# An interaction network whose products are formed with field pairs on partitions instead of samples, so that no product tile is transposed

## The chip, the cores and the metric

The kernel runs on one core of a Trainium2 chip. The metric is device time in microseconds (us), the median of several runs. The engines are named as in the profile: PE is TensorE (matmul), PEld its weight loads, DVE is VectorE, ACT is ScalarE, POOL is GpSimd, SP is SyncE, which here only issues DMAs. All data is float32. A product of two float32 matrices is made from float32r matmuls: each operand is split into a high part (rounded to float32r) and a low part (the rest).

## The reference

1024 samples, 39 fields each. `inputs` is [1024, 39, 16]: an embedding row looked up in a table, times the field's value. With h = `inputs` at first, three layers are computed, each for every embedding column d (16 of them):

```
x = einsum('bhd,bmd->bhmd', h, inputs).reshape(B, -1, 16)   # all pairs (h, m)
x = relu(einsum('bcd,oc->bod', x, W_i) + b_i)               # 200 outputs
h, direct = x[:, :100], x[:, 100:]                          # last layer: direct = x
```

The first layer has 39*39 pairs (the kernel uses their symmetry: 780), the second and third 100*39 = 3900 each. The `direct` parts are summed over d and dotted with `fc_W`. Beside it a dense network 624 -> 400 -> 400 with relu runs on the flat inputs, is dotted with the rest of `fc_W`, and a bias per looked-up row is added. The output is one score per sample.

## The kernel before

The samples are cut into 8 tiles of 128, and each tile into its 16 columns d: 128 chunks. A chunk's layer is a matmul with the products as the stationary operand, [pairs on partitions, 128 samples], and the weights as the moving one; it needs 7 tiles of 128 pairs in layer 0 and 31 tiles in each of layers 1 and 2.

POOL forms the products with the samples on partitions (`product0`, `product`), so they have the wrong orientation for the matmul. Layer 0 products are transposed on PE (`turn_group`); those of layers 1 and 2 on DVE, in blocks of 32 x 32 (`turn_group` of the DVE program, L719). For that h and the inputs are held "quartered": 32 samples on each quarter of the partitions, which ACT prepares with 16 small copies per layer (`quarter`, L598).

A transposed group (4 tiles, 128x512) lies in PSUM. ACT copies it to `xhi` (`high`, L582), DVE subtracts to get `xlo` (`low`, L725), and PE does two matmuls per tile (`multiply_group`): L524, xhi against [high | low] weights, 400 columns, and L525, xlo against the high weights, 200 columns. One group each of layers 1 and 2 is left "whole": 4 tiles by plain float32 matmuls (L516). `low_copy`, `add` and `dot` clear an accumulator and feed the next layer.

Every engine runs one hand-written order. In step i they do layer 0 of chunk i+1, layer 1 of chunk i and layer 2 of chunk i-1 (`step_groups`), with rings of 4 buffers. POOL also gathers the next sample tile's 39 embedding rows, 2 or 3 indirect DMAs at the head of each step (`gathers`, L364), and scales them once a tile. After the last chunk comes the dense network.

Of the kernel before, what the change touches and what calls it, by code (L numbers as in the profile page):

```python
# [55 lines left out]
SPLIT_GROUPS = [GROUPS[0], GROUPS[1] - 1, GROUPS[2] - 1]  # L77
STEP = sum(SPLIT_GROUPS)
LAST = CHUNKS - 1
DENSE_STEP = GROUPS[FIRST] + GROUPS[SECOND]  # L80
CIN_GROUPS = STEP * CHUNKS
assert STEP % RING == 0 and DENSE_STEP % RING == 0


def first_group(i):

    return 2 * SPLIT_GROUPS[0] + SPLIT_GROUPS[1] + STEP * (i - 1)


def dense_group(i):  # L90

    return CIN_GROUPS + GROUPS[FIRST] + DENSE_STEP * (i - 1)


SLOT = first_group(1) % RING
DENSE_SLOT = dense_group(1) % RING


def groups_of(job, c):
    return [(job, c, q) for q in range(GROUPS[job])]  # L100


def whole(job, q):

    return job in (1, 2) and q == WHOLE[job]


def splits_in(groups):
    return sum(1 for job, c, q in groups if not whole(job, q))
# [7 lines left out]
L0_DONE = 4  # L117
L1_DONE = 9


def dense_groups(i):
    return groups_of(FIRST, i) + groups_of(SECOND, i - 1)


def group_tiles(job, q):

    return range(SIZE[job] * q, min(SIZE[job] * (q + 1), len(ROWS[job])))


def group_parts(job, q):  # L130

    parts = []
    for t in group_tiles(job, q):
        at = (t % SIZE[job]) * P
        if parts and parts[-1][0] == ROWS[job][t]:
            parts[-1] = (parts[-1][0], slice(parts[-1][1].start, at + P))
        else:
            parts.append((ROWS[job][t], slice(at, at + P)))
    return parts


def weights_at(layer, t):

    before = sum(KT[n] - (GROUP if WHOLE[n] is not None else 0) for n in range(layer))
    skipped = WHOLE[layer] is not None and t >= GROUP * (WHOLE[layer] + 1)
    return (before + t - (GROUP if skipped else 0)) * 2 * OUTS


def start_groups():
    return groups_of(0, 0) + groups_of(0, 1) + groups_of(1, 0)  # L150


def is_first(c):
    return isinstance(c, int) and c == 0


def tail_groups():

    return groups_of(1, LAST) + groups_of(2, LAST - 1) + groups_of(2, LAST) + groups_of(FIRST, 0) + dense_groups(1)


def rec_kernel(nc, x_store, vals, ids, table, w0_ab, w0_ba, w1, w2, d0, d0_b, d1, d1_b, fc_w, fc_b, out):
    with ExitStack() as ctx:
# [6 lines left out]

        W = sb("W", [P, weights_at(2, KT[2])], F32R)
        w_whole = sb("w_whole", [P, 2, GROUP, OUTS], F32)
        x_whole = sb("x_whole", [P, 2, GROUP * P], F32)
        prods = sb("prods", [P, KT_ALL * P], F32)
        xhi = sb("xhi", [P, RING, GROUP * P], F32R)
        xlo = sb("xlo", [P, RING, GROUP * P], F32R)
# [79 lines left out]
        s_out = sem("output_stored")  # L256

        block = ctx.enter_context(nc.Block())

        per = STAGE // OUTS
# [649 lines left out]
```

## Time and profile before

| | |
|---|---|
| median of 3 runs | 3019.55 us (3016.03 to 3020.39) |
| the profiled execution: time, span | 3024.12 us, 3022.3 us |
| granted PE clock, mean | 0.996 |
| PE / PEld busy | 95% / 92% |
| DVE / ACT / POOL busy | 90% / 72% / 80% |
| data moved by DMA | 29.42 MB, mean 10 GB/s |

An engine's share is the time in which it ran an instruction. The span is from the first to the last instruction; the profiled execution's time is 1.8 us longer. Matmuls overlap each other, so what a matmul costs is read from the distance between two starts and not from its duration; on DVE and ACT too the next instruction starts up to 0.1 us before the last one's end.

### The profile page before, as it was taken

To read this page: it belongs to the slowest core of one execution; us is meant where nothing else is said; L and a number is where in the kernel's file an instruction comes from. 1 tells how busy PE (TensorE), PEld (TensorE's weight loads), DVE (VectorE), ACT (ScalarE), POOL (GpSimd) and SP (SyncE) were. 2 spreads that over 40 slices of the span, in tenths; PEclk is the share of its full clock that TensorE was granted. 3 is DMA by queue.
4 is the path that set the end of the run, shared out by engine and by line. 5 is a ranking of instruction groups with operands and counts; after the bars stand their busy time and mean duration, and the time that the engine had idled before them with its cause. 6 is when DMAs were issued, how large, how long until landed. Compare 5 with 4: busy or idle time off the path is not lost.

```text
span 3022.3 us, 69958 instructions
## 1 busy us (share of the span) xinstructions
PE 2883.5 (95%) x18848; PEld 2783.5 (92%) x18848; DVE 2731.5 (90%) x5355; ACT 2163.4 (72%) x6593; POOL 2417.9 (80%) x1513
## 2 busy tenths in 40 slices
PE   0799999999999999999999999999999999999998
PEld 0799999999999999999999999999999999999997
DVE  2699999999999999999999999999999999999995
ACT  2677777777777777777777777777777777777772
POOL 7788888888888888888888888888888888767660
PEclk9899999999999999999999999999999999999999
DMA  6100010000000010000100001000100001000001
GB/s 122 19 1 1 1 22 1 1 1 7 16 1 1 1 22 1 1 1 1 22 1 1 1 1 22 1 1 1 21 2 1 1 1 22 1 0 0 0 35 30
DMA packets 36455, 29.42 MB, mean 10 GB/s; under 512 B 22960, under 2 KB 28976, under 8 KB 36400
## 3 DMA queue, kind: packets, MB, share of 16 engines
q1 hardware_dynamic: 26160, 26.11, 3.8%
q0 software_dynamic: 10240, 2.81, 3.2%
q14 instruction: 48, 0.39, 0.0%
q8 instruction: 7, 0.11, 0.0%
HBM read 26.33 MB, written 2.56 MB: 10 GB/s over the span
## 4 chain that ended last, share of the span: by engine, by line
ACT 30%; issue 29%; DVE 29%; PE 6%; DVEq 2%; ACTq 2%; POOL 2%; DMA 1%; SPq 0%; POOLq 0%
DVE xlo L725 15%; ACT h2q L598 10%; ACT h1q L598 10%; ACT xhi L582 10%; DVE turn L719 7%; DVE acc_sum L735 4%; PE acc L524 2%; DVE x_whole L719 2%; POOL raw L364 1%; DVEq L723 1%; ACTq L580 1%; PE acc L525 1%; DVE spent L742 1%; PE turn L496 1%; PE acc L516 1%
## 5 line engine op out<-in xcount | busy, mean ns | idle before, releaser
L524 PE MATMUL acc<-W,xhi 128*128 128x400 f32 x7808 | 2437.0, 374 | 61.3 <-DVE xlo L725 36.0
L525 PE MATMUL acc<-W,xlo 128*128 128x200 f32 x7808 | 1990.3, 255 | 0.0
L524 PEld LDWEIGHTS acc<-W,xhi 128*128 128x128 f32 x7808 | 1467.5, 188 | 154.5 <-DVE xlo L725 153.5
L725 DVE TENSOR_TENSOR xlo<-turn,xhi 128x512 fp32r<-128x512 f32 (+1 forms) x2088 | 1341.7, 648 | 223.7 <-ACT xhi L582 194.6
L525 PEld LDWEIGHTS acc<-W,xlo 128*128 128x128 f32 x7808 | 1492.1, 191 | 0.0
L582 ACT ACTIVATE xhi<-turn 128x512 fp32r<-128x512 f32 (+1 forms) x2088 | 1165.4, 571 | 397.9 <-PE acc L525 216.2
L414 POOL TENSOR_TENSOR prods<-h1q,xq 128x1092 f32<-128x1092 f32 (+2 forms) x512 | 933.1, 1854 | 413.7 <-ACT h1q L598 407.2
L719 DVE STREAM_TRANSPOSE turn<-prods 128x512 f32<-128x512 f32 (+1 forms) x1792 | 1244.9, 695 | 18.3 <-POOL prods L414 13.3
L414 POOL TENSOR_TENSOR prods<-h2q,xq 128x1092 f32<-128x1092 f32 (+2 forms) x512 | 934.1, 1854 | 12.6 <-ACT h2q L598 12.6
L598 ACT ACTIVATE h1q<-acc_sum 32x25 f32<-32x25 f32 x2048 | 456.2, 223 | 242.5 <-DVE acc_sum L735 215.1
L598 ACT ACTIVATE h2q<-acc_sum 32x25 f32<-32x25 f32 x2048 | 456.9, 223 | 76.9 <-DVE acc_sum L735 49.6
L516 PE MATMUL acc<-w_whole,x_whole 128*128 128x200 f32 x2048 | 393.0, 335 | 0.0
L364 POOL DMA_INDIRECT raw<-table,idx x320 | 313.4, 979 | 89.4 <-issue 82.3
L516 PEld LDWEIGHTS acc<-w_whole,x_whole 128*128 128x128 f32 x2048 | 336.4, 190 | 0.0
L397 POOL TENSOR_TENSOR prods<-xin 128x780 f32 (+1 forms) x128 | 215.5, 1684 | 5.2 <-POOL idx L359 3.1
L496 PE MATMUL turn<-ident,prods 128*128 128x128 f32 (+1 forms) x928 | 146.0, 275 | 69.1 <-POOL prods L397 67.8
L589 ACT ACTIVATE acc_lo<-acc 128x200 f32<-128x200 f32 x384 | 129.2, 337 | 96.7 <-PE acc L525 96.7
L719 DVE STREAM_TRANSPOSE x_whole<-prods 128x512 f32<-128x512 f32 x256 | 177.3, 693 | 0.0
L496 PEld LDWEIGHTS turn<-ident,prods 128*128 128x128 f32 (+1 forms) x928 | 105.6, 141 | 71.7 <-issue 68.3
L735 DVE TENSOR_TENSOR acc_sum<-acc,acc_lo 128x200 f32<-128x200 f32 x384 | 135.2, 352 | 10.4 <-ACT acc_lo L589 10.4
L742 DVE SCALAR_TENSOR_TENSOR spent<-acc_sum,fcp 128x100 f32<-128x100 f32 (+1 forms) x384 | 105.5, 275 | 0.1
L742 DVE DVE_READ_ACCUMULATOR spent<-acc_sum,fcp (+1 forms) x384 | 32.6, 85 | 0.0
(44 smaller groups left out, 227.5 us busy)
## 6 DMA issues: line engine op xcount, KB each, us to landing
xq<-x_store SPq DMA_DIRECT2D x32, 312.0 KB
raw<-table,idx POOLq DMA_INDIRECT x320
prods<-w SPq DMA_DIRECT2D x9, 500.0 KB, 7.8
x_store<-xin SPq DMA_DIRECT2D x8, 312.0 KB
raw<-x_store SPq DMA_DIRECT2D x8, 312.0 KB, 2.9
prods<-d SPq DMA_DIRECT2D x1, 1000.0 KB, 4.8
w_whole<-w SPq DMA_DIRECT2D x2, 400.0 KB, 12.8
prods<-d SPq DMA_DIRECT2D x1, 800.0 KB, 6.5
```

Source lines behind the costliest of these rows:

```text
L364: nc.gpsimd.indirect_dma_start(out=raw[:, m * EMB_COLS:(m + 1) * EMB_COLS], out_offset=None, in_=table, in_offset=bass.IndirectOffsetOnAxi ...
L397: nc.gpsimd.tensor_tensor(prods[:, 0:PAIRS].rearrange("p (s a) -> p s a", a=FIELDS), x[:, 0:FIELDS].unsqueeze(1).broadcast_to([P, SHIFTS, ...
L414: nc.gpsimd.tensor_tensor(out[:, :, a * FIELDS:b * FIELDS].rearrange("p q (h m) -> p q h m", m=FIELDS), hq[layer - 1][:, :, a:b].unsqueeze ...
L496: mm = pe.transpose(turn[slot][0:rows, at:at + P], src[:, t * P:t * P + rows], ident[:])
L516: mm = pe.matmul(bank[:, 0:OUTS], x_whole[:, job - 1, at:at + P], w_whole[:, job - 1, t % GROUP, :], start=False, stop=False, skip_group_c ...
L524: pe.matmul(bank[:, 0:2 * OUTS], hi, w, start=start, stop=end, skip_group_check=True)
L525: mm = pe.matmul(bank[:, 0:OUTS], lo, w[:, 0:OUTS], start=False, stop=end, skip_group_check=True)
L582: op = nc.scalar.activation(xhi[0:rows, slot, cols], turn[slot][0:rows, cols], ACT.Copy)
L598: op = nc.scalar.activation(hq[layer][QUARTER * i:QUARTER * (i + 1), q, :], acc_sum[QUARTER * q:QUARTER * (q + 1), layer, H_QUARTER * i:H_ ...
L719: nc.vector.transpose(place.rearrange("p (t q s) -> p t q s", q=4, s=QUARTER), src.rearrange("p q (t k) -> p t q k", k=QUARTER)).then_inc( ...
L725: op = nc.vector.tensor_tensor(xlo[0:rows, slot, cols], turn[slot][0:rows, cols], xhi[0:rows, slot, cols].bitcast(F32), ALU.subtract)
L735: nc.vector.tensor_tensor(acc_sum[:, layer, :], acc[layer][:, 0:OUTS], acc_lo[:, layer, :], ALU.add).then_inc(s_acc[layer], 1)
```

## The change

The products are now formed with the pairs on partitions: partition p holds h number p, and the free dimension runs over fields m and samples. Both factors have to be spread for it.

The inputs go through memory. DVE turns a scaled tile (`turn_inputs`), SP stores it by field (`store_inputs`, to `xs`), and from there reads it back for each chunk so that every partition gets the same rows: 96 partitions read the same 4 KB, 32 others a second piece (`load_block`, four blocks per chunk into `xrep`, double-buffered), and `load_layer0`. That is 31 x 128 samples x 4 bytes on each of 128 partitions for a chunk, 2.03 MB, and 0.48 MB more for layer 0. The dense network reads its inputs by field, too. The weights are rearranged to the new order of rows through memory at the start.

h needs one transpose on PE per layer and chunk (`turn`), between two copies on ACT: `take` before it and `spread` (six activations) behind it.

The groups are shared out. Two of 4 tiles per layer ("P", 3 tiles in the second one of layer 0) are multiplied and made low by POOL, six more per layer ("D") by DVE, with the product in PSUM; ACT makes every high part. All tiles are split now and the whole groups are gone; a tile that holds the left-over rows has its low part on its own spare partitions and needs one matmul of 400 columns. Rings: 3 buffers for P, 4 for D, 3 PSUM banks.

```
-def step_groups(i):
-    l0, l1 = groups_of(0, i + 1), groups_of(1, i)
-    return l0[:1] + l1[:3] + l0[1:] + l1[3:] + groups_of(2, i - 1)
+ORDER = [("P", 0), ("D", 0), ("D", 1), ("P", 1), ("D", 2), ("D", 3), ("P", 2), ("D", 4), ("D", 5), ("P", 3),
+         ("D", 6), ("D", 7), ("P", 4), ("D", 8), ("D", 9), ("P", 5), ("D", 10), ("D", 11)]
...
+            def load_block(c, buf, e):      # SP
+                sp.dma_start(xrep[0:H_MAIN, buf, t0:t0 + n, :].rearrange("p t n -> p (t n)"),
+                             field_rows(c, t0, n).partition_broadcast(H_MAIN)).then_inc(s_xblk[e], 16)
...
+            def low(i, k):                  # POOL; product(i, par, k) writes prod_p
+                n, slot, cols = p_num(i, k), p_slot(i, k), len(tiles_of("P", k)) * P
+                pool.wait_ge(s_hi_p, n + 1)
+                nc.gpsimd.tensor_tensor(xlo_p[:, slot, 0:cols], prod_p[:, slot, 0:cols],
+                                        xhi_p[:, slot, 0:cols].bitcast(F32), ALU.subtract).then_inc(s_lo_p, 1)
...
+                for at, k in enumerate(mine):            # POOL, one step
+                    if at + 1 < len(mine):
+                        product(i, par, mine[at + 1])
+                    elif ahead is not None:
+                        product(i + 1, 1 - par, ahead)
+                    low(i, k)
...
+            with pool.Fori(0, TILES - 1) as k:
+                for j in range(DIM):
+                    gathers(j)
+                    if j == FREE_AT:
+                        scale(k + 1, True)
+                        copy_idx((k + 2) % TILES, k + 3)
+                    step(k * DIM + (j + 2), j % 2, 0)
...
+                for kind, g in step_order(i):            # PE, one step
+                    multiply(i, kind, g)
+                    if (kind, g) == ("D", 1) and not (isinstance(i, int) and i < 1):
+                        turn(1, i - 1, i - 1)
+                    if (kind, g) == ("D", 7) and 0 in layers:
+                        turn(0, i + 1, i)
...
+            def spread(l, c, i):            # ACT
+                act.wait_ge(s_turn[l], c + 1)
+                h = hrep[l][:, 0, :]
+                nc.scalar.activation(hrep[l][0:H_MAIN, 2:4, :],
+                                     h[0:H_MAIN, :].unsqueeze(1).broadcast_to([H_MAIN, 2, P]), ACT.Copy)
+                nc.scalar.activation(hrep[l][H_MAIN:P, 3, :], h[QUARTER:2 * QUARTER, :], ACT.Copy)
+                nc.scalar.activation(hrep_s[l][0:H_MAIN, :], h[0:H_MAIN, :], ACT.Copy)
+                nc.scalar.activation(hrep_s[l][H_MAIN:P, :], h[0:QUARTER, :], ACT.Copy)
+                nc.scalar.activation(hrep[l][H_MAIN:P, 2, :], h[2 * QUARTER:3 * QUARTER, :], ACT.Copy)
+                nc.scalar.activation(hrep[l][0:P - 4, 1, :], h[0:P - 4, :], ACT.Copy).then_inc(s_hrep[l], 1)
...
+                    if (kind, g) == ("D", 3) and 1 in layers and inner:    # ACT, behind high(i, kind, g)
+                        spread(1, i - 1, i - 1)
+                    if (kind, g) == ("D", 9) and 0 in layers:
+                        spread(0, i + 1, i)
```

Two places of the order matter for what follows. On POOL, before, the boundary of two steps (h1q and h2q are h of layers 1 and 2, quartered; the DMAs are the gathers):

```order
L414 TENSOR_TENSOR prods<-h2q,xq 128x4x234 [waits turned2]
L414 TENSOR_TENSOR prods<-h2q,xq 128x4x195 [waits turned2]
L364 DMA raw<-table,idx 128x17 x2
L393 ISA
L397 ISA [waits turned0]
L397 TENSOR_TENSOR prods<-xin 128x780
L403 ISA
L412 ISA [waits h1_quartered]
L414 ISA [waits turned1]
L414 TENSOR_TENSOR prods<-h1q,xq 128x4x273
L412 REGISTER_ALU
```

And now, at the same boundary (prod_p<-l0x 128x512 is group P0 of the next step, 128x384 is P1; xlo_p is the low part, first of P4, then of P5, and last of P0):

```order
L529 REGISTER_ALU
L530 TENSOR_TENSOR xlo_p<-prod_p,xhi_p 128x512 [waits p_high]
L510 ISA
L517 ISA [waits layer0_inputs_loaded]
L524 TENSOR_TENSOR prod_p<-l0x 128x512 [waits p_low]
L529 REGISTER_ALU
L530 TENSOR_TENSOR xlo_p<-prod_p,xhi_p 128x512 [waits p_high]
L484 DMA raw<-table,idx 128x17 x2
L517 REGISTER_ALU
L524 TENSOR_TENSOR prod_p<-l0x 128x384 [waits p_low]
L529 REGISTER_ALU
L530 TENSOR_TENSOR xlo_p<-prod_p,xhi_p 128x512 [waits p_high]
```

The gathers still stand at the boundary, but the low parts of P5 and P0 now stand around them, and each waits for ACT's high part.

On ACT, before, behind the low copy of layer 0, where h goes to layer 1:

```order
L586 REGISTER_ALU
L589 ACTIVATE acc_lo<-acc 128x200 [waits acc_summed0,split_group_multiplied]
L594 REGISTER_ALU
L596 REGISTER_ALU [waits acc_summed0]
L598 ACTIVATE h1q<-acc_sum 32x25 [waits products1]
L598 ACTIVATE h1q<-acc_sum 32x25 x3
L578 REGISTER_ALU
L582 ACTIVATE xhi<-turn 128x384 [waits split_group_multiplied,turned1]
L598 ACTIVATE h1q<-acc_sum 32x25 [waits products1,acc_summed0]
```

And now, from the high part of D9 on (hrep and hrep_s are h as spread, waiting for PE's transpose; then the high parts of P5 and D10, and `take` of layer 1):

```order
L738 ACTIVATE xhi_d<-prod_d 128x512 [waits d_multiplied,d_products]
L768 ACTIVATE hrep<-hrep 96x256 [waits p_products,h1_turned]
L770 ACTIVATE hrep<-hrep 32x128
L771 ACTIVATE hrep_s<-hrep 96x128
L772 ACTIVATE hrep_s<-hrep 32x128
L773 ACTIVATE hrep<-hrep 32x128
L774 ACTIVATE hrep<-hrep 124x128
L729 REGISTER_ALU
L732 ACTIVATE xhi_p<-prod_p 128x512 [waits p_multiplied,p_products]
L735 REGISTER_ALU
L738 ACTIVATE xhi_d<-prod_d 128x512 [waits d_multiplied,d_products]
L757 ACTIVATE hbuf<-acc 128x96 [waits h2_turned,fc_dotted1]
```

The high part of P5 now stands behind six copies that wait for a transpose on PE; before, the copies of h waited for DVE's sum only and stood between groups.

## Rows read from the trace of the kernel before

**Rows 1.** Stretch, us; busy of PE, PEld, DVE, ACT, POOL; clock; DMA share; GB/s.

```profile
10.00:20.00 10.00, 0.00 (x0) 0.00 (x0) 8.50 (x9) 6.21 (x8) 8.12 (x7) 1.00 0.98 262
40.00:60.00 20.00, 0.00 (x0) 0.00 (x0) 0.00 (x0) 0.00 (x0) 15.12 (x17) 1.00 0.20 7
107.00:2944.00 2837.00, 2796.02 (x18375) 2704.19 (x18373) 2654.51 (x5198) 2110.95 (x6472) 2340.78 (x1441) 1.00 0.05 6
2944.00:3022.30 78.30, 65.58 (x366) 58.47 (x364) 42.70 (x101) 23.37 (x58) 3.66 (x3) 0.94 0.10 29
```

**Rows 2.** Waits of the steady part, 107 to 2944 us: total, times, longest.

```profile
POOL prods L414 <- ACT h1q L598: 403.0, 123, 7.4
...
PEld acc L524 <- DVE xlo L725: 131.9, 380, 2.5
```

**Rows 3.** Timeline of PE in the steady part: start us, us, then what ran.

```profile
1504.52 1.53 PE L516 MATMUL acc<-w_whole,x_whole 128*128 128x200 f32 x8
1505.75 0.48 PE L524 MATMUL acc<-W,xhi 128*128 128x400 f32 x1
...
1518.64 0.49 PE L496 MATMUL turn<-ident,prods 128*128 128x128 f32 x3
1518.88 0.43 PE L524 MATMUL acc<-W,xhi 128*128 128x400 f32 x1
...
1522.17 0.36 PE L524 MATMUL acc<-W,xhi 128*128 128x400 f32 x1
1522.37 0.26 PE L525 MATMUL acc<-W,xlo 128*128 128x200 f32 x1
...
1525.10 0.36 PE L524 MATMUL acc<-W,xhi 128*128 128x400 f32 x1
...
1526.86 1.54 PE L516 MATMUL acc<-w_whole,x_whole 128*128 128x200 f32 x8
```

**Rows 4.** Timeline of DVE, same stretch.

```profile
1499.92 0.67 DVE L725 TENSOR_TENSOR xlo<-turn,xhi 128x512 fp32r<-128x512 f32 x1
1500.52 0.68 DVE L719 STREAM_TRANSPOSE x_whole<-prods 128x512 f32<-128x512 f32 x1
...
1518.84 0.35 DVE L735 TENSOR_TENSOR acc_sum<-acc,acc_lo 128x200 f32<-128x200 f32 x1
```

**Rows 5.** Timeline of ACT, same stretch.

```profile
1503.23 0.93 ACT L598 ACTIVATE h1q<-acc_sum 32x25 f32<-32x25 f32 x4 [1.70 <-DVE acc_sum L735]
...
1509.14 0.33 ACT L589 ACTIVATE acc_lo<-acc 128x200 f32<-128x200 f32 x1
1509.36 0.61 ACT L582 ACTIVATE xhi<-turn 128x512 fp32r<-128x512 f32 x1
...
1519.24 0.50 ACT L582 ACTIVATE xhi<-turn 128x384 fp32r<-128x384 f32 x1 [0.67 <-PE turn L496]
```

**Rows 6.** Groups of POOL instructions by shape: busy us, mean ns of one.

```profile
L414 POOL TENSOR_TENSOR prods<-h1q,xq 128x1092 f32<-128x1092 f32 x256 | 520.0, 2053 | 413.7 <-ACT h1q L598 407.2 <-DMA xq<-x_store 6.5
...
L397 POOL TENSOR_TENSOR prods<-xin 128x780 f32 x125 | 210.5, 1684 | 4.8 <-POOL idx L359 3.1
L414 POOL TENSOR_TENSOR prods<-h1q,xq 128x780 f32<-128x780 f32 x128 | 194.7, 1521 | 0.0
...
L374 POOL TENSOR_TENSOR xin<-raw,val 128x624 f32 x7 | 13.1, 1873 | 0.0
```

**Rows 7.** Timeline of POOL, same stretch as ACT.

```profile
1499.73 1.53 POOL L414 TENSOR_TENSOR prods<-h2q,xq 128x780 f32<-128x780 f32 x1
...
1504.93 1.69 POOL L397 TENSOR_TENSOR prods<-xin 128x780 f32 x1
...
1516.28 7.23 POOL L414 TENSOR_TENSOR prods<-h2q,xq 128x1092 f32<-128x1092 f32 x4
...
1525.92 1.68 POOL L397 TENSOR_TENSOR prods<-xin 128x780 f32 x1
```

**Rows 8.** Chain of waits in the start-up: start us, us, what.

```profile
67.64 8.38 DMA x_store<-xin
```

More of the change, by code:

```diff
@@ L130, in group_parts @@
[L130 to L146, printed above, removed]
@@ L344, in _ @@
+            sp.wait_ge(s_prod_p, p_num(CHUNKS, 5) + 1)
+            sp.wait_ge(s_prod_d, d_num(CHUNKS, 11) + 1)
+            for tile in range(2, TILES):
                 load_dense(tile)
@@ L533, in multiply_group @@
-                mm.then_inc(s_mmw[job] if whole(job, q) else s_mm, 1)
-            def run(n0, slot0, groups, ahead, fresh=False, distance=2):
-                following = groups + ahead
-                def turn_ahead(g):
-                    if g < len(following) and following[g][0] not in (1, 2):
-                        before = splits_in(following[:g])
-                        turn_group(n0 + before, (slot0 + before) % RING, *following[g])
-                if fresh:
-                    for g in range(2):
-                        turn_ahead(g)
-                for g in range(len(groups)):
-                    turn_ahead(g + distance)
-                    before = splits_in(groups[:g])
-                    multiply_group(n0 + before, (slot0 + before) % RING, *groups[g])
+                        mm = split_tile(acc[layer], hi, lo, w, start, end)
@@ L588, in low_copy @@
+            def low_copy(layer, c, i):
+                if layer == 2:
+                    act.wait_ge(s_mm_d, d_num(i, 11) + 1)
+                else:
+                    act.wait_ge(s_mm_p, p_num(i, 1 + 2 * layer) + 1)
+                if some(c):
                     act.wait_ge(s_acc[layer], c)
@@ new lines, in step @@
+            def step(i, par, ahead):
+                layers, mine = present(i), d_groups(i)
+                for at, d in enumerate(mine):
+                    if at + 2 < len(mine):
+                        product(i, par, mine[at + 2])
+                    elif at + 2 - len(mine) < len(ahead):
+                        product(i + 1, 1 - par, ahead[at + 2 - len(mine)])
+                    low(i, d)
+                    if d == 3 and 1 in layers and not (isinstance(i, int) and i < 2):
+                        evacuate(2, i - 2)
+                    if d == 5 and 0 in layers:
+                        evacuate(0, i + 1)
+                    if d == 9 and 1 in layers:
+                        evacuate(1, i)
+                if layers == (0, 1):
+                    evacuate(1, i)
@@ new lines, in _ @@
+            with dve.Fori(0, TILES - 1) as k:
+                for j in range(DIM):
+                    if j == 8:
+                        turn_inputs(k + 1, True)
+                    step(k * DIM + (j + 2), j % 2, [0, 1])
+            for i in range(2 + DIM * (TILES - 1), CHUNKS):
+                step(i, i % 2, d_groups(i + 1)[0:2] if i < LAST else [])
+            evacuate(2, LAST - 1)
+            product(CHUNKS, 0, d_groups(CHUNKS)[0])
+            product(CHUNKS, 0, d_groups(CHUNKS)[1])
```

1132 lines of the change are left out of this document (654 added, 478 removed).

## The prediction

> **What bounds the kernel now.** I read the busy time by stretch first, then the waits of the steady part, then the timelines of one step. In the steady part, 107 to 2944 us, PE is busy 2796 of 2837 us, DVE 2655, POOL 2341, ACT 2111 [rows 1]; the largest wait is POOL's for h1q, 403 us, and PE's weight loads wait 132 us for DVE's low parts [rows 2]. So PE is nearly full, and DVE is close behind it. One step is the distance between the two whole groups of layer 1, 1504.52 and 1526.86: 22.34 us [rows 3]. What PE needs for it comes from distances of starts: ten pairs (L524, L525) take 1525.10 - 1522.17 = 2.93 us, 0.293 a pair; a whole group takes 1505.75 - 1504.52 = 1.23; three transposes 0.24 [rows 3]. 61 pairs, two whole groups and seven transposes make 17.9 + 2.5 + 0.6 = 20.9 us, and 1.4 us a step are gaps.
>
> **What PE does after the change.** 67 pairs (7 + 30 + 30), two matmuls of 400 columns without a partner at 0.20 each (1522.37 - 1522.17), and two transposes at 0.08: 19.6 + 0.4 + 0.2 = 20.2 us [rows 3]. The work removed (two whole groups and five transposes, 2.5 + 0.4) is nearly paid back by six more pairs and the two lone matmuls (1.8 + 0.4). If nothing else counted, a step would lose 2.1 us.
>
> **What the other engines do.** DVE: 24 instructions of 512 elements or fewer, 0.60 us apart at most (1499.92 to 1500.52), and three evacuations of an add, 0.35, and a dot of the like [rows 4]: 14.4 + 2.1 = 16.5 us. That a product reads and writes PSUM is shown by no row; the nearest are the subtraction and the transpose of the same size at 0.67 and 0.68, and DVE has 4 us to spare, so I cost it at nothing. ACT: 18 high parts at 0.6 or less, three low copies at 0.33, four copies in `take` and twelve in `spread`. Four copies of 25 elements took 0.93 and a copy of 200 let the next start after 0.22 [rows 5], so 0.23 each: 10.8 + 1.0 + 3.7 = 15.5 us. POOL: twelve instructions of 512 or 384 elements. No row has that size. Rows 6 give 2053 ns for 1092 and 1521 for 780 elements, 1.7 ns an element and 0.19 us fixed, so 1.06 us; the product of layer 0, both inputs streaming, 1684 for 780, gives 1.17; the strided scaling, 1873 for 624, gives 3.0 ns an element and 1.54. The new operands are contiguous; I take 1.1 and keep 1.0 and 1.54 as ends. With 2.44 gathers at 1.25 a step that is 13.2 + 3.0, about 16.5 with the scaling. Each engine has less to do than PE's 20.2. What decides is then the order.
>
> The GPSIMD Engine Reference of the Trainium skill (3.1, Elementwise — side-by-side cycle accounting) says that a two-input `tensor_tensor` on this engine costs about 2.6 cycles an element at 1.2 GHz. The rows give 1.7 to 1.9 ns where the rule gives 2.2. By the rule one instruction would be 1.27 us, an estimate from that page, and the sum 3270 us.
>
> **The wait that the change adds.** Count from the moment when PE has issued D7 and turns h1 (t = 0). ACT's `spread` waits for that transpose, the high part of P5 is queued behind it on ACT, and POOL's low part of P5 behind that. Transpose 0.4 (three took 0.49 [rows 3]), six copies 6 * 0.23 + 0.1 = 1.5, high part 0.6 [rows 5], low part 1.1, and three hand-overs at 0.1 (transposes end at 1519.13, ACT starts at 1519.24 [rows 3, 5]): P5 is ready at 3.9. Meanwhile PE has P4, D8 and D9, 12 pairs, 3.5 us. Gap 0.4.
>
> Behind the low part of P5 POOL has the gathers of the next step, the product of P1, and only then the low part of P0, with which PE begins the next step. Three gathers take from 1501.26 (1499.73 + 1.53) to 1504.93, 3.67 us, two from 1523.51 to 1525.92, 2.41 [rows 7]. So P0 is ready at 3.9 + 3.67 + 2 * 1.1 + 0.1 = 9.9, or 8.6 with two gathers, or 6.2 with none. PE wants it after P5, D10 and D11, ten pairs and a lone matmul: 3.9 + 2.9 + 0.2 = 7.0. Gap 2.9, 1.6 or none. Nothing catches it up: the next turn again waits for PE's own D7, so a gap of one step is not made good in the next.
>
> The turn of h2 has the same chain to P2: ready at 3.9, while PE has only P1, D2 and D3, 11 pairs, 3.2. Gap 0.7. For the other groups I walked the same orders and found the low parts about 1 us or more ahead of PE (P3 is the closest).
>
> Steps: 20.2 + 0.4 + 0.7 = 21.3 without gathers, 22.9 with two, 24.2 with three. Of 16 steps of a sample tile nine have three and six have two (39 gathers over 15 steps); the last has the scaling, one of 1.87 [rows 6], one of about half that, and small ones, 3.9 in all, so 24.4. Mean (9 * 24.2 + 6 * 22.9 + 24.4) / 16 = 23.7, against 22.34 now.
>
> **The DMAs.** SP issues 14 a step. They bring 2.03 + 0.48 = 2.5 MB; at the 262 GB/s of the start-up, where the queues are 98% full [rows 1], that is 9.6 us of 23.7. Each block is asked for some five D groups, about 8 us, before its first product, and a block of 0.52 MB takes 2 us to move, so I cost them at nothing. Their limit: below 2.5 MB / 23.7 us = 106 GB/s they become the bound. They also share the engines with the gathers. With the queues 98% full 7 gathers were issued in 10 us, 1.43 each, against 17 in 20 us in the quiet stretch, about 1.2 [rows 1]. At half load that is at most 0.1 per gather; I leave it in the range.
>
> **Start and end.** Full steps are 126 before and after. The rest is now 3022.3 - 126 * 22.34 = 207 us. The end keeps its work (the last groups, the dense layers; 78.3 us from 2944 [rows 1]). The start gets longer. All 7.7 MB of weights go to memory in the new order and come back: 15.4 MB at 262 GB/s are 59 us, beside the first gathers, which end at about 60 anyhow. Then the inputs are stored in 3840 pieces of 128 bytes, where 2048 pieces of 156 took 8.4 us [rows 8], so 7 us more; 22 instead of 4 DMAs spread them and the layer-0 and block loads follow, 9 more; and the halves of layers 1 and 2 (6200 columns each, at DVE's 0.60 / 512 some 7 us) are now made between the first steps, 14 us. I take 30, with 0 and 60 as ends.
>
> **Sum.** 112 steps of the loop with gathers, 14 without (the first one and the last sample tile's): 112 * 23.7 + 14 * 21.3 + 207 + 30 = 2654 + 298 + 237 = 3189 us of span. The profiled execution was 1.8 us over its span and 4.6 over the median, so 3186; I say 3185. Ends: POOL's 1.0 instead of 1.1 shortens a step by 0.4 us and the start by up to 30, giving 3110; gathers at 1.35 and the longer start give 3250. With the hand-overs 0.1 either way the likeliest case has 3080 to 3290.
>
> **Rivals.**
> - *The gathers stay hidden* (faster). POOL runs ahead far enough that its 3 to 4 us at the step boundary don't reach PE: 126 * 21.3 + 237 = 2921 us, or 2820 if the turns cost nothing either. For it: every engine's load is under 17 of 20.2 us, and the gathers before were harmless beside a POOL that waited 403 us [rows 2]. Against it: the low part of P5 cannot be made before `spread`, by the rows of the order. The break-even step is (3022 - 237) / 126 = 22.1 us, a mean gap of 1.9 where I count 3.5; half of my error would do. Chance 0.30, a third of it between 2921 and 3013.
> - *POOL is dearer than thought* (slower still). At 1.54 us per instruction three of them stand on the way to P0, two of them new behind the gathers, and one on the way to P2: 25.5 us with gathers, 22.3 without, 112 * 25.5 + 14 * 22.3 + 237 = 3405. For it: the scaling's row; against: its inputs are strided. Chance 0.11.
> - *The broadcast reads are slow* (slower). 16 queues read the same 4 KB; no row of before shows that in a steady stream. At 90 GB/s a step would last 28 us and the kernel 126 * 28 + 237 = 3765. Chance 0.04.
> - *No change within what can be told* (0.2%, 6 us): 0.03, where gains and gaps happen to cancel.
>
> **How the numbers follow.** My forecast has 0.52. Slower by over 0.2%: 0.52 + 0.11 + 0.04 = 0.67; faster 0.30; the same 0.03. Below 2920 lie about 0.1 and above 3380 about 0.1, so the range is 2920 to 3380.
>
> **What the profile after would show.** Right: PE waits for POOL's xlo_p, some 300 us in all; the step is 24 us with three gathers and near 21.3 in the last sample tile, which has none, and this difference is the clearest sign. POOL is idle before the low part of P5 and busy behind it. ACT's first hrep copy waits for PE's transpose twice a step. POOL's 512-element instructions take 1.0 to 1.2 us; DMA is near half busy. Wrong: steps with and without gathers equally long; PE waiting for DVE's xlo_d, which would mean that the product in PSUM is slow; DVE or POOL waiting for xrep; a first full step later than 180 us. If the steps with gathers are under 22 us, the forecast fails, most likely at the walk from the turn to P0.

## The result, and the profile after

The changed kernel takes 3377.57 us (median of 4 runs, 3369.05 to 3378.28); the kernel before, on the same chip, 3019.97 (3016.03 to 3020.49). The ratio is 1.118, 95% interval 1.116 to 1.120. The forecast was 3185 us, with a range of 2920 to 3380: the sign was right, the time lies at the upper end of the range, and the kernel lost 358 us where 165 were forecast. The profiled execution has a span of 3375.5 us.

First the busy time by stretch, with the columns of [rows 1]. The first line is the steady part (from the first full step to the last), the others look into one step.

```profile
169.00:3307.00 3138.00, 2743.98 (x17504) 2649.58 (x17503) 2195.05 (x4442) 1738.54 (x4684) 2122.18 (x1817) 0.97 0.41 107
...
1515.00:1520.00 5.00, 3.38 (x21) 3.12 (x21) 4.55 (x8) 1.53 (x4) 4.25 (x5) 1.00 0.16 6
1520.00:1522.00 2.00, 1.02 (x3) 1.03 (x4) 1.18 (x3) 1.46 (x4) 2.00 (x2) 0.63 0.30 89
1522.00:1524.00 2.00, 2.00 (x9) 1.99 (x9) 1.32 (x5) 0.00 (x0) 2.00 (x3) 0.50 0.51 150
1524.00:1526.00 2.00, 2.00 (x9) 1.99 (x8) 0.00 (x0) 0.00 (x0) 0.29 (x1) 0.50 0.00 2
1526.00:1528.00 2.00, 2.00 (x12) 2.00 (x11) 0.00 (x0) 0.08 (x1) 0.00 (x0) 0.66 0.00 0
1528.00:1530.00 2.00, 2.00 (x16) 2.00 (x16) 0.34 (x1) 1.92 (x7) 0.00 (x0) 1.00 0.00 0
```

PE was busy 2796 of 2837 us before and is busy 2744 of 3138 now. No engine is full, so the order decides. What PE has to do is what the forecast said (e2 below has steps of 20.18 us); the gaps are larger. The last column but two has something new: behind the gap at 1518 to 1521 us the granted clock is 0.50, that is 1.2 GHz, for 6.8 us.

The waits of the whole execution (total, times, longest), which answer to [rows 2]:

```profile
POOL xlo_p L530 <- ACT xhi_p L732: 911.7, 252, 12.5
ACT hrep L768 <- PE hrep L639: 726.4, 255, 6.5
DVE prod_d L915 <- ACT hrep L774: 625.9, 247, 6.2
PE acc L606 <- POOL xlo_p L530: 528.6, 369, 110.0
...
DVE prod_d L915 <- DMA xrep<-xs: 32.4, 7, 5.1
```

Read from the bottom: DVE hardly waits for the broadcast loads. PE waits for POOL's low parts, POOL for ACT's high parts, ACT for the turn on PE, twice a step. This is the ring of the forecast.

POOL in one step with three gathers (start us, us, what; what ended the idle time), to be held against [rows 7]:

```profile
1509.16 1.29 POOL L524 TENSOR_TENSOR prod_p<-l0x 128x512 f32<-128x512 f32 x1
1513.70 1.29 POOL L530 TENSOR_TENSOR xlo_p<-prod_p,xhi_p 128x512 fp32r<-128x512 f32 x1 [3.25 <-ACT xhi_p L732]
1515.13 0.98 POOL L484 DMA_INDIRECT raw<-table,idx  x1
...
1518.62 1.01 POOL L524 TENSOR_TENSOR prod_p<-l0x 128x384 f32<-128x384 f32 x1
1519.57 1.27 POOL L530 TENSOR_TENSOR xlo_p<-prod_p,xhi_p 128x512 fp32r<-128x512 f32 x1
```

ACT in the same step: six copies of the spread, and only then the high part of P5.

```profile
1511.25 0.36 ACT L768 ACTIVATE hrep<-hrep 96x256 f32<-96x256 f32 x1 [1.63 <-PE hrep L639]
...
1512.70 0.26 ACT L774 ACTIVATE hrep<-hrep 124x128 f32<-124x128 f32 x1
1512.99 0.63 ACT L732 ACTIVATE xhi_p<-prod_p 128x512 fp32r<-128x512 f32 x1
```

And PE, from the turn to the first group of the next step:

```profile
1510.95 0.27 PE L639 MATMUL hrep<-ident,hbuf 128*128 128x128 f32 x1
...
1518.06 0.36 PE L628 MATMUL acc<-W,xhi_d 128*128 128x400 f32 x1
1520.98 0.70 PE L606 MATMUL acc<-W,xhi_p 128*128 128x400 f32 x1 [2.56 <-POOL xlo_p L530]
...
1521.64 0.59 PE L606 MATMUL acc<-W,xhi_p 128*128 128x400 f32 x1
...
1522.19 0.58 PE L606 MATMUL acc<-W,xhi_p 128*128 128x400 f32 x1
```

The reader sees the forecast's walk: P5 ready 1514.99 - 1510.95 = 4.0 us after the turn (forecast 3.9), P0 started after 10.0 (9.9), the gap 2.56 (2.9). What the forecast did not have is the distance of the pairs behind the gap: 0.55 us instead of 0.29.

The length of a step is the distance between the starts of ACT's copy L768 for h1. Two steps:

```profile
1412.44 0.36 ACT L768 ACTIVATE hrep<-hrep 96x256 f32<-96x256 f32 x1 [1.63 <-PE hrep L639]
...
1435.73 0.36 ACT L768 ACTIVATE hrep<-hrep 96x256 f32<-96x256 f32 x1 [1.63 <-PE hrep L639]
...
3165.86 0.36 ACT L768 ACTIVATE hrep<-hrep 96x256 f32<-96x256 f32 x1 [1.63 <-PE hrep L639]
...
3187.56 0.36 ACT L768 ACTIVATE hrep<-hrep 96x256 f32<-96x256 f32 x1 [1.63 <-PE hrep L639]
```

23.3 us with two gathers, 21.7 without any (in the last sample tile). I measured all steps in this way. All 42 with two gathers take 23.3 (forecast 22.9). The 63 with three take 24.5 at least (24.2), but 36 of them 26.0 to 31.0. The seven with the scaling take 26.2 to 26.4 (24.4), the last 13 21.7 (21.3). The loop's 112 steps take 2808.5 us, mean 25.08, where the forecast had 23.7.

### The profile page after: what moved, and what is told of

It reads as the page before. It is cut to its first block, busy times and chain, and to the rows that moved or that the text cites. A ratio compares the mean times of both kernels' runs of the same rounds, so it can differ in the third digit from the quotient of the medians.

```text
span 3375.5 us, 66460 instructions
## 1 busy us (share of the span) xinstructions
PE 2824.3 (84%) x17912; PEld 2723.2 (81%) x17912; DVE 2265.5 (67%) x4563; ACT 1790.0 (53%) x4774; POOL 2231.5 (66%) x1921
## 4 chain that ended last, share of the span: by engine, by line
issue 44%; POOL 39%; PE 7%; SPq 6%; DVE 2%; ACT 1%; DMA 1%; POOLq 1%; ACTq 0%; DVEq 0%
POOL xlo_p L530 17%; POOL prod_p L524 16%; POOL raw L484 5%; PE acc L606 4%; SPq L351 3%; PE acc L607 2%; DMA l0x<-xs 1%; SPq L291 1%; DVE xlo_d L923 1%; DVE prod_d L915 0%; SPq L314 0%; POOL xin L497 0%; POOLq L517 0%; SPq L301 0%; SPq L367 0%
## 5 line engine op out<-in xcount | busy, mean ns | idle before, releaser
L606 PE MATMUL acc<-W,xhi_d 128*128 128x400 f32 x5632 | 1770.5, 373 | 13.8 <-DVE xlo_d L923 11.6
L530 POOL TENSOR_TENSOR xlo_p<-prod_p,xhi_p 128x512 fp32r<-128x512 f32 (+1 forms) x768 | 953.7, 1242 | 911.7 <-ACT xhi_p L732 911.7
L915 DVE TENSOR_TENSOR prod_d<-hrep,xrep 128x512 f32<-128x512 f32 (+1 forms) x1536 | 1039.0, 677 | 719.2 <-ACT hrep L774 625.9
L607 PE MATMUL acc<-W,xlo_d 128*128 128x200 f32 x5632 | 1462.2, 260 | 0.0
L606 PE MATMUL acc<-W,xhi_p 128*128 128x400 f32 x2944 | 993.5, 388 | 528.6 <-POOL xlo_p L530 528.6
L607 PEld LDWEIGHTS acc<-W,xlo_d 128*128 128x128 f32 x5632 | 1113.6, 198 | 0.0
L606 PEld LDWEIGHTS acc<-W,xhi_d 128*128 128x128 f32 x5632 | 1095.6, 195 | 18.2 <-DVE xlo_d L923 13.3
L923 DVE TENSOR_TENSOR xlo_d<-prod_d,xhi_d 128x512 fp32r<-128x512 f32 (+1 forms) x1536 | 982.0, 639 | 170.2 <-ACT xhi_d L738 166.0
L738 ACT ACTIVATE xhi_d<-prod_d 128x512 fp32r<-128x512 f32 (+1 forms) x1536 | 886.7, 581 | 54.7 <-DVE prod_d L915 25.6
L607 PE MATMUL acc<-W,xlo_p 128*128 128x200 f32 x2944 | 764.6, 260 | 0.0
L524 POOL TENSOR_TENSOR prod_p<-hrep_s,xrep 128x512 f32<-128x512 f32 x512 | 664.8, 1298 | 15.5 <-ACT hrep L774 8.3
L768 ACT ACTIVATE hrep<-hrep 96x256 f32<-96x256 f32 x256 | 92.4, 361 | 726.4 <-PE hrep L639 726.4
L628 PE MATMUL acc<-W,xhi_d 128*128 128x400 f32 x256 | 92.6, 362 | 0.0
```

The lines of the kernel that those rows point to most:

```text
L524: nc.gpsimd.tensor_tensor(to, one.unsqueeze(1).broadcast_to([P, count, P]), many, ALU.mult).then_inc(s_prod_p, 1)
L530: nc.gpsimd.tensor_tensor(xlo_p[:, slot, 0:cols], prod_p[:, slot, 0:cols], xhi_p[:, slot, 0:cols].bitcast(F32), ALU.subtract).then_inc(s_l ...
L606: pe.matmul(bank[:, 0:2 * OUTS], hi, w, start=first, stop=last, skip_group_check=True)
L607: return pe.matmul(bank[:, 0:OUTS], lo, w[:, 0:OUTS], start=False, stop=last, skip_group_check=True)
L738: nc.scalar.activation(xhi_d[:, slot, 0:cols], prod_d[d_bank(i, g)][:, 0:cols], ACT.Copy).then_inc(s_hi_d, 1)
L915: nc.vector.tensor_tensor(to, h, xrep[:, (par + layer - 1) % 2, a:a + count, :], ALU.mult).then_inc(s_prod_d, 1)
```

## Experiments

All are changes of the changed kernel, if nothing else is said: e6 is one of the kernel before, e8 stands on e2, e9 on e8, and e10 and e12 on e9. "Steps" are measured as above, and long ones at single places of the loop are told in the text.

| run | median us | ratio to before (95%) | steps: two / three gathers / none, us | 112 loop steps, us |
|---|---|---|---|---|
| changed kernel | 3377.57 | 1.116 to 1.120 | 23.3 / 24.5+ / 21.7 | 2808.5 |
| e11 no second rewrite | 3372.05 | 1.110 to 1.118 | 23.3 / 24.5+ / 21.7 | 2826.9 |
| e4 clock kept | 3341.73 | 1.104 to 1.108 | 23.3 / 24.5 / 23.3 | 2758.9 |
| e13 short product | 3289.92 | 1.087 to 1.091 | 22.8 / 24.0+ / 21.7 | 2719.8 |
| e1 gathers moved | 3165.21 | 1.046 to 1.050 | 21.7 / 22.1 / 21.7 | 2590.6 |
| e5 no gathers | 3076.37 | 1.017 to 1.020 | - / - / 21.7 | 2502.7 |
| e7 h1's high part first | 3043.54 | 1.006 to 1.009 | 21.1 / 21.3 / 21.1 | 2476.0 |
| e3 both edits | 3024.27 | 1.001 to 1.002 | 20.2 / 21.2 / 20.2 | 2474.1 |
| e2 both high parts first | 2935.27 | 0.970 to 0.973 | 20.2 / 20.4 / 20.2 | 2384.6 |
| e8 stores split | 2878.72 | 0.952 to 0.955 | 20.2 / 20.4 / 20.2 | 2326.2 |
| e10 gathers late | 2877.38 | 0.952 to 0.955 | 20.2 / 21.0 / 20.2 | 2335.1 |
| e9 start reordered | 2864.57 | 0.948 to 0.951 | 20.2 / 20.4 / 20.2 | 2323.3 |
| e12 first gathers late | 2848.31 | 0.942 to 0.944 | 20.2 / 20.4 / 20.2 | 2302.2 |

**e1: the gathers at another place of POOL's row.**

```
-    gathers(j)
     ...
-    step(k * DIM + (j + 2), j % 2, 0)
+    step(k * DIM + (j + 2), j % 2, 0, lambda: gathers(j))   # called ahead of low(i, 5)
```

> POOL issues the gathers of the loop just ahead of its low part of P5, where it stands idle for 3.25 us in the trace after, instead of just ahead of the product of P1. Theory (the gathers lie behind the spread on the way to P0, and the gap lets PE's clock fall): the low part of P0 is ready 2.4 to 3.7 us earlier in the steps with gathers, they fall from 25.1 us in the mean to 21.5 to 22.5, and granted clocks of 0.50 in the loop go; 112 * 3.1 = 350 us less, about 3030 us, with 2960 and 3130 as ends. Rival A (every gather costs by what it moves or by load on the DMA queues, wherever it stands): steps stay at 24 to 25, 3330 to 3380. Rival B (the dearer POOL instructions bind by their sum): steps about 24, over 3250.

3165 us. Steps with two gathers fell from 23.3 to 21.7, with three from 24.5 to 22.1: two gathers vanish in POOL's idle 3.25 us, three stick out of it by 0.4. The fallen clock goes from all of these; 16 stretches at 0.50 are left in the loop, instead of 43, behind its 16 long steps. Rivals A and B are out. These 16 steps of 28.6 to 30.9 us are also why the total missed the theory's 3030 (ends 2960 and 3130): seven are those of the scaling, which now waits for the rows of gathers that were issued later (14.8 us in all), seven wait for the layer-0 rows (46.0 us, see e8), and in two a gather stands 6 us (see e12).

**e2: the spread behind the high part.**

```
-    if (kind, g) == ("D", 3) and 1 in layers and inner:
+    if (kind, g) == ("P", 2) and 1 in layers and inner:
         spread(1, i - 1, i - 1)
-    if (kind, g) == ("D", 9) and 0 in layers:
+    if (kind, g) == ("P", 5) and 0 in layers:
         spread(0, i + 1, i)
```

> ACT makes the high part of P2 ahead of the spread of h2, and that of P5 ahead of the spread of h1, instead of behind them; the gathers stay where they are. Theory (the spread pins the low part of P5, and all of POOL's row behind it): POOL makes the low part of P5 some 2.3 us earlier, so the gathers and the low part of P0 come 2.3 us earlier too, and the gap at P2 goes; steps with three gathers about 22 to 22.5, with two about 21.5, no fall of the clock; about 3040 us, with 2970 and 3140 as ends. Rival (the hrep copies come so late now that the products wait for them, or POOL's sum binds): steps stay over 23.5, over 3200.

2935 us, 85 less than the kernel before, and below the theory's ends (2970 and 3140). The gathers stand where they stood, and all but 15 steps of the loop take 20.2 to 20.7 us: just what the forecast gave PE to do, 20.2. The rival, steps over 23.5, is out. POOL of this kernel, around the gathers that end at 1508.2:

```profile
1508.18 1.02 POOL L524 TENSOR_TENSOR prod_p<-l0x 128x384 f32<-128x384 f32 x1
1509.15 1.29 POOL L530 TENSOR_TENSOR xlo_p<-prod_p,xhi_p 128x512 fp32r<-128x512 f32 x1
...
1522.37 1.30 POOL L524 TENSOR_TENSOR prod_p<-l0x 128x512 f32<-128x512 f32 x1
1523.63 1.29 POOL L530 TENSOR_TENSOR xlo_p<-prod_p,xhi_p 128x512 fp32r<-128x512 f32 x1
1525.07 0.98 POOL L484 DMA_INDIRECT raw<-table,idx  x1
```

The low part of P5 follows the product without the 3.25 us of idle time, before the turn of h1 is even spread (ACT's copy L768 starts at 1524.42); the theory had it 2.3 us earlier, and it no longer waits for the turn at all. So the two pinned low parts, of P2 and P5, were the whole loss of the changed kernel against the kernel before, and more.

**e3: both edits.**

> Both edits at once: gathers ahead of the low part of P5, and the high parts of P2 and P5 ahead of the spreads. Theory: no gap at the boundary is left, the step is what PE needs plus small gaps, 20.5 to 21.3 us with and without gathers; 126 * 20.9 + 263 = 2900, with 2850 and 2970 as ends, faster than the kernel before. Rival (one edit alone already takes all that can be had): the same as the better of the two single edits. Rival (another bound stands at 22 to 23 us, by POOL's sum or DMA): over 3030.

3024 us: worse than e2 alone. None of the three cases came: neither the theory's 2900, nor the better of the two single edits, nor a step of 22 to 23 us. What I had not written is this: when the low part of P5 is no longer late, three gathers ahead of it make it late (21.2 us a step instead of 20.4), and the scaling waits as in e1 (28.0 to 29.2 us instead of 20.7, 55 of the 90 us that the loop loses against e2). A place that is free in one order isn't free in the other.

**e7: only the spread of h1 behind.**

> Only the spread of h1 goes behind the high part of P5; the spread of h2 stays ahead of the high part of P2. Theory: P0 comes in time, the gap at P2 stays; by the forecast that gap is 0.7 us, by the trace after it is a part of the 1.5 us between 21.7 and 20.2, so steps of 20.9 to 21.4 with and without gathers, no fall of the clock but at the stalls: 2935 + 126 * 0.9 = 3050 us, with 3020 and 3090 as ends. Rival (the gap at P2 is the larger one and its delay runs on into the next turn): over 3150. Rival (the gap at P2 costs nothing once P0 is in time): 2935 to 2950.

3043.5 us, as the theory had it (3050); of the 442 us of e2, 334 come from this half of the edit alone. Without gathers a step is 21.13 us. Against 20.18 in e2 and 21.69 in the changed kernel this prices the two gaps of the forecast: at P2 0.95 us (forecast 0.7), at P5 0.56 (0.4).

**e5 and e6: the loop's gathers left out, after and before.**

```
 for j in range(DIM):
-    gathers(j)
```

> The changed kernel without the gathers of its loop (those ahead of the loop stay; the inputs of most later sample tiles are then stale). Theory (in the loop the gathers stand behind the pinned low part of P5, on the way to P0, and the clock falls behind the gaps they make): all 126 full steps last 21.7 us as the last 13 do in the trace after, save the ones where SP or POOL stalls at the loop's boundary; 112 * 3.4 = 380 us less, 3000 us, with 2980 and 3050 as ends. Rival (the last steps are short because no block or store of a later tile is loaded beside them, and the gathers are innocent): steps over 23, over 3150.

> The kernel before without the gathers of its loop. Theory (there POOL had slack and nothing waited behind the gathers): no more than 30 us less than before, 2990 to 3020. Rival (the gathers cost in both kernels, the change only added a constant): 150 us or more less, under 2870.

After: 3076 us, 301 less. Before: 3019.4 against 3019.3, ratio 0.9988 to 1.0007: nothing. The waits of before without gathers say why; POOL's wait for h1q is 745 us instead of the 403 to 407 of [rows 2, 6], so all that the gathers took was idle time:

```profile
POOL prods L416 <- ACT h1q L599: 745.4, 127, 7.4
```

So the same gathers are free in one kernel and cost 300 us in the other. The forecast had 112 * 23.7 - (105 * 21.3 + 7 * 24.4) = 247 us for them. The e5 total is 76 above the 3000 I expected, and above the end of 3050, since 20 steps of its loop take 22.8 to 27.9 us: seven with the scaling, seven in which POOL waits for the layer-0 rows, and six at the head of a pass of the loop. These seven with the rows are 30 us over the usual here; in the changed kernel they are only 6 us over it, so there the gaps of the gathers covered most of that wait.

**e4: the gap filled with matmuls without effect.**

```
+    if (kind, g) == ("P", 0) and not isinstance(i, int):
+        pe.wait_ge(s_hbuf[0], i + 1)
+        for _ in range(14):
+            pe.matmul(acc[0][:, 2 * OUTS:512], ident_r[:, 0:P], ident_r[:, 0:112],
+                      start=False, stop=False, skip_group_check=True)
     multiply(i, kind, g)
```

> Everything as in the changed kernel, but in the loop PE issues 14 matmuls of 112 columns on data without effect ahead of P0, before it waits for the low part of P0 (the results of layer 0 are not the reference's, since the accumulator's unused columns are written). Theory (a part of the time is not the gap itself but PE's clock of 0.50 behind it): the granted clock stays at 1.00 in the loop, the steps of 24.9 us and more at j other than 0 fall to 24.5 or a little less, 80 to 120 us less, about 3280. Rival (the clock is no cause, the long steps come from something else, such as DMA latency of the gathers): within 20 us of 3377.

3341.7 us, 36 less, not 80 to 120. Two things are in it. In the loop the steps with three gathers that had taken 26 to 27.5 us take 24.5, save seven at 26.1: 45 us less. The seven with the scaling fall from 26.3 to 24.7: 11 us less. The others lose 2 and gain 8, so the 112 steps take 49.6 us less, and the stretches at 0.50 are 17 instead of 43. PE's own loop goes on into the last sample tile, and in 12 of its steps, which have no gathers, the 14 matmuls stand in the way and cost 1.6 us each, some 19 us. In this stretch of e4 the gap is filled and the clock stays at full speed:

```profile
1520.00:1530.00 10.00, 9.67 (x69) 9.43 (x69) 8.39 (x16) 4.72 (x12) 8.96 (x8) 1.00 0.38 88
```

So the fallen clock is a cause of its own, worth 56 us at least in these steps (the long ones at the head of a pass took 29.5 to 30.6 us here too).

**e13: one POOL instruction shorter.**

```
-    a, count = tiles[0], len(tiles)
+    a, count = tiles[0], 1 if k == 1 and not isinstance(i, int) else len(tiles)
```

> The changed kernel, but in the loop POOL forms only the first 128 of the 384 columns of the product of P1 (the others keep what stood there, so layer 0 is not the reference's). This instruction stands behind the gathers and ahead of the low part of P0, took 1.01 us and should take about 0.4. Theory (in the steps with gathers each us on that row is a us of the step, in those without it is none): steps with three gathers fall from 24.5 to 23.9, with two from 23.3 to 22.7, the last 13 stay at 21.7; 112 * 0.6 = 67 us, and with the gap at 2.0 instead of 2.6 us some of the 50 us that the fallen clock costs goes too: 3377 - 90 = 3287 us, with 3255 and 3312 as ends. Rival (POOL's instructions are not the limit there, what they wait for is): under 20 us.

3290 us; the forecast of the theory was 3287. Its instruction, before (of the changed kernel) and in e13, from the groups by shape:

```profile
L524 POOL TENSOR_TENSOR prod_p<-l0x 128x384 f32<-128x384 f32 x128 | 129.6, 1012 | 3.5 <-POOL idx L479 1.7
```

```profile
L524 POOL TENSOR_TENSOR prod_p<-l0x 128x128 f32<-128x128 f32 x112 | 52.4, 468 | 3.5 <-POOL idx L479 1.7
```

0.54 us less, and the steps with gathers lose 0.55 each, so on this row a us of POOL is a us of the step. Over the 112 steps that is 62 us of the 89 that the loop lost; the stretches at 0.50 are 31 instead of 43. What the edit says nothing of is the steps without gathers: in the last 13, which stay at 21.7, the product was not shortened (112 of 128 were). That a shorter instruction on another row would be worth nothing, no run here tests.

**e8: SP's stores in portions.** In e2 every 16th step still took 28.1 to 28.9 us, with POOL waiting, 8.46 us in the one below, for the layer-0 rows. SP of e2 at such a place:

```profile
390.27 17.56 SPq L351 DMA_DIRECT2D xe<-xs  x20
408.09 0.57 SPq L353 DMA_DIRECT2D xe<-xs  x1
408.90 0.56 SPq L355 DMA_DIRECT2D x_store<-xs  x1
409.84 0.34 SPq L367 DMA_DIRECT2D l0x<-xs  x1
```

```
-    if j == 10:
-        spread_inputs(k + 1)
+    if 10 <= j < 14:
+        then = lambda: spread_inputs(k + 1, [j - 10])   # behind load_layer0
```

> Both spreads behind the high parts, and besides: SP's 22 DMAs that write xe, which stand in one row for 17.6 us once a sample tile and delay the layer-0 loads behind them (steps of 28 us at every 16th place), go in four portions behind the layer-0 loads of four steps; at the start they go behind the layer-0 loads and three block loads. Theory: seven steps of 28.5 become 20.4 (57 us), and the first matmul comes some 16 us earlier; 2935 - 57 - 16 = 2862 us, with 2845 and 2890 as ends. Rival (the DMA queues, not SP's row, delay the layer-0 load, so the long steps stay): 2915 to 2935.

2878.7 us. The seven long steps are 20.4 now, and 56.6 us are gone, the 57 of the theory; but nothing of the 16 us at the start. The first matmul came at 100.5 us instead of the 111.9 of e2, and then step 1 waited 21.4 us for rows that SP now loads behind layer 2's weights. SP's row of issues, not the DMA engines (0.43 busy from 390 to 408 us in e2), was the limit. The Trainium skill (DMA: Bandwidth & Descriptors, "Issuing engines are not separate DMA queues") calls the time to start a DMA usually small beside the transfer. Here it was not: 20 of them held the queue for 17.6 us, 0.88 each, where at the 262 GB/s of [rows 1] their 64 KB would move in 0.25 us (an estimate), and what stood behind them cost 8 us a tile.

**e9, e10, e12: the start, and the gathers once more.**

```
 split_weights(0)
-step(-1)
 split_weights(1)
+step(-1)
```

(and on POOL the gathers of tile 1 behind the first steps, on SP `load_layer0(2)` ahead of `load_weights(2, w2)`.)

> The kernel with both spreads behind the high parts and the stores split (2878.7 us), with its start in another order: the 21 gathers of tile 1, which stand ahead of the first layer-0 product on POOL, go behind step -1 and step 0; ACT and DVE split layer 1's weights while they wait, ahead of step -1; SP loads layer 0's rows of chunk 2 ahead of layer 2's weights, where POOL waited 21 us for them. Theory (in the start these rows of work stand one behind another, not the DMA queues' bytes): the steady steps begin 15 to 25 us earlier, 2858 us, with 2850 and 2867 as ends. Rival (the start is bound by the bytes that its queues move, 99% busy up to 140 us): within 6 us of 2879.

2864.6 us (2861.7 to 2870.9), 14 less: nearly the theory's 15 to 25, and outside the rival's 6. The loop begins 12 us earlier. ACT now waits 11.4 us for layer 2's weights.

> As the start reordered, and in the loop the gathers go behind the low part of P0 instead of ahead of the product of P1. Theory (once in 16 steps, and at two places more, a gather waits 3.8 to 6 us for nothing the profile shows; that delays P0 now, and behind P0 a part of it is covered): the eight long steps of 25.6 to 28.4 us lose 2 to 4 us each, 20 to 30 us less than the start reordered alone. Rival (P1 then comes late instead, by as much): within 6 us of it; or slower, where three gathers push P1 behind its need in every step: 40 us more.

2877.4 us, 13 more. Six of the eight long steps fell from 25.4-26.1 to 22.1, as expected, the other two only from 28.0 and 27.2 to 26.2 and 26.8; but the steps with three gathers take 21.0 instead of 20.4. Both the theory and its rival were right, and the rival was larger.

> As the start reordered (2864.6 us), but of the loop's gathers only those of its first step (j = 0) go behind the low part of P0; the others stay ahead of the product of P1. Theory: a gather waits once in 16 steps, at the loop's start, and late there it costs 22.1 instead of 25.6 us, seven times or, with the first, six, while the other steps keep 20.4: 20 to 25 us less, 2842 us, with 2838 and 2850 as ends. Rival (the long wait moves on to the next gathers ahead of P1): within 6 us of 2864.6.

2848.3 us (2844.7 to 2851.9), 16 less than e9 where 20 to 25 were expected; ratio to the kernel before 0.943. It is the best version of the study. The wait that it covers, in POOL of e8:

```profile
1516.94 0.99 POOL L494 DMA_INDIRECT raw<-table,idx  x1 [3.84 <-issue]
```

"issue" means that the profile shows nothing that the engine waited for. In e8 it comes six times at the first gather of a pass of the loop, and at two gathers elsewhere. The theory of e10 and e12 took both for a wait of the gathers. For the six that is wrong: e5 has no gathers in its loop, and there the same wait stands ahead of the first product of the pass, and so it does in e12 and e1:

```profile
1619.86 1.00 POOL L525 TENSOR_TENSOR prod_p<-l0x 128x384 f32<-128x384 f32 x1 [1.93 <-issue]
```

It belongs to the head of the pass, whatever instruction stands first there (1.9 to 3.3 us in e5, 2.9 to 3.3 in e12, six times each). The DMA view shows something beside it. A queue that it calls "instruction" moves six packets around each of these heads; in the changed kernel, from 1787.5 to 1792 us, beside a wait that ends at 1790.4, it has these (packets, MB, share), and elsewhere in its loop three in a row at most:

```profile
q14 instruction: 6, 0.05, 3.9%
```

That POOL waits for them fits, but no run shows it. What e12 gained it gained because the three gathers no longer stand behind this wait on the way to P0. The two waits elsewhere do go with the gathers: they are in the kernel before too (3.8 and 3.3 us), without such packets beside them, and in neither e5 nor e6. What ends them stays open.

**e11: the second rewrite of weights left out.**

> The changed kernel without the eight DMAs that write layer 2's weights to memory in the new order (layer 2 is computed with layer 1's weights instead; everything else is loaded as before). They take SP from 18.5 to 37.6 us, and their bytes the queues. Theory (SP's row and full queues make the start late, as far as the sample's rows are not ready before 71 us anyhow): the first matmul at 95 to 104 instead of 110, 6 to 15 us less in all, 3362 to 3372. Rival (the bytes bind: 3.8 MB read and written at 262 GB/s are some 29 us): 25 us less or more. Rival (the gathers, which POOL issues up to 58 us, bind the start): no change.

3372 us (3346.6 to 3393.0; the changed kernel 3369 to 3378). The first matmul came at 101.7 us instead of 110.0, 8.3 earlier, as the theory had it, and the loop began 8.4 us earlier; both rivals are out for the start. The total can't tell it: in the profiled execution the loop took 2826.9 us instead of 2808.5, though it is the same loop, through other steps with a fallen clock. Executions of this one program differ by 46 us.

## Why the forecast was right in sign and too low in size

**The work of PE: right.** 20.2 us; e2 shows steps of 20.18.

**The walk from the turn of h1 to P0: right.** 3.9 and 9.9 us forecast, 4.0 and 10.0 measured. Steps of 21.3, 22.9 and 24.2 became 21.7, 23.3 and 24.5 where nothing else disturbed them. That the walk is off by only 0.1 us is a little luck. "I take 1.1" for a POOL instruction was wrong:

```profile
L530 POOL TENSOR_TENSOR xlo_p<-prod_p,xhi_p 128x512 fp32r<-128x512 f32 x640 | 825.3, 1290 | 905.7 <-ACT xhi_p L732 905.7
```

1.29 us, which is 0.19 more, twice on the way from the turn to P0. The Trainium skill's rule (GPSIMD Engine Reference, 3.1, Elementwise — side-by-side cycle accounting), about 2.6 cycles an element, is 2.17 ns at 1.2 GHz, and the runs agree with it: products of 128, 384 and 512 columns took 468 (e13), 1012 and 1296 ns, which is 2.1 to 2.2 ns an element and 0.19 us fixed. The rule alone gives 1.11 us for 512; the 1.27 of the forecast has 0.16 of a fixed part in it. I had taken the price per element from rows with one operand repeated [rows 6], 1.7 ns; the row with both inputs streaming, 1684 ns for 780, pointed the right way and lost. That the repetition made the old rows cheap is not shown: the new products repeat one operand too, 128 columns for each of 4 tiles, and cost as much as the low parts, which repeat none (1298 and 1290 ns). Against it the third instruction on the way has 384 columns and took 1.01, and the three gathers took 3.49 us (1515.13 to 1518.62) instead of 3.67, which took back most of it.

**The turn of h2: right, too small.** 0.95 us instead of 0.7 (e7). **The turn of h1 at P5: right, too small.** 0.56 instead of 0.4.

**The products in PSUM at nothing: right.** 699 ns each, and in the steady part PE and its weight loads wait 9 us in all for DVE's low parts. **The DMAs at nothing: right for the DMA engines, wrong for SP's row.** That each block is asked for some five D groups ahead held, save in seven steps, where DVE waited up to 5.1 us for xrep; that 22 stores a tile stand in one row ahead of the layer-0 loads was in my count of the start only. In the changed kernel this cost little (6 us beyond the usual 24.5 in seven steps), because the gaps covered it; in e2 it was 57 us.

**The step that failed: the mean of the loop's steps, "Mean (9 * 24.2 + 6 * 22.9 + 24.4) / 16 = 23.7".** It took a gap at its length, 2.9 us, with PE at full speed behind it, and let every step with three gathers cost the same. It had no term for the clock behind the gap and none for the waits of POOL that "issue" stands for. The runs show 25.1 in place of 23.7. Of the loop's 151 us (2808.5 against 112 * 23.72 = 2657):

- 36 us: the base, 0.3 us in 63 steps and 0.4 in 42.
- 56 us: the fallen clock, the 48 other steps with three gathers beyond their 24.5 (e4 took 45 of it away).
- 40 us: eight steps of 28.5 to 31.0, six at the head of a pass and two at a gather, in which POOL waits for nothing that is shown, and the clock falls behind it too.
- 13 us: the scaling, 26.3 instead of 24.4; 11 of these are the fallen clock again (e4: 24.7).
- 6 us: SP's stores.

The last 13 steps give 5 more. **Start and end:** I took 30 us more, with 60 as the end, and it was 57 (285 us outside of the 125 steps of loop and last tile, instead of 237 and a step of 21.3, is 27 more). Of this some 8 us are one rewrite of weights in SP's row (e11, whose loop begins 8.4 us earlier), and some 12 the order of the start (e9 beside e8, on another kernel); the rest is not taken apart. 151 + 5 + 27 + 3 of rounding the mean = 186 of the 186.5 us between the span and the 3189 of the sum.

**The rivals.** "The gathers stay hidden" was wrong as the kernel stood, but only by the order of two instructions on ACT: its 2921 us is what e2 reached (2935). "POOL is dearer" named 3405 us and came nearest in time for the wrong reason: the instruction is 1.29, not 1.54. The broadcast reads are not slow: at 107 GB/s DVE waits for xrep 32 us in all. Of the signs that I had listed, three showed: steps with and without gathers differ, ACT waits for the turn twice a step, and POOL is idle before the low part of P5; 300 us of PE's wait for xlo_p were 388 in the steady part alone. Of the signs of being wrong DVE's wait for xrep showed, 32 us in seven steps.

## What to carry to other kernels

A queue on an in-order engine is only as early as its most pinned instruction: look for copies that wait for a turn of the data and stand ahead of work that doesn't need it, and let that work go first. Two lines on ACT were worth 442 us here, more than the 358 that the whole change cost. A gap in PE costs more than its length once the clock falls behind it: where a forecast has gaps of this size (2.6 us here), the slow pairs behind them belong in the sum. And after each mend look again: the wait behind SP's stores had been hidden, 6 us in the changed kernel and 57 in e2.

## What the runs showed that I had not expected

- PE was idle 2.56 us, and the granted clock fell to 0.50 (1.2 GHz) behind it. The loop of the changed kernel has 43 stretches at 0.50, 3.4 to 6.8 us long. The steps with two gathers never show one: all 42 take 23.3. Of the 48 undisturbed steps with three gathers 26 do. In e11, whose loop is the same, it isn't the same ones, and the times of that one program spread by 46 us.
- The first instruction of POOL in a pass of the loop stood 1.9 to 5.1 us without a shown reason, from the second pass on, be it a gather (e8) or a product (e1, e5, e12); in e3, 1.5 at most. Two gathers elsewhere in the loop stood 3.2 to 6.7 us, in every kernel here that has them; also in e8, whose DMA engines were half idle.
- SP issued the 20 stores of 64 KB and less at 0.88 us each in the quiet loop, where a block load of 384 KB took 0.32.
